# Thirty-four unread products in four places of TensorE's order, in a post-norm attention and ternary FFN kernel

## What is computed

```python
def step(carry, inp):                     # over the 8 segments of 128 tokens
    mem, z = carry
    sq = elu(q) + 1;  att_mem = sq @ mem / (sq @ z)
    sk = elu(k) + 1;  mem = mem + sk^T v;  z = z + sum(sk)
    att = softmax(q k^T * scale) @ v
    return (mem, z), gate * att_mem + (1 - gate) * att
x = layernorm(x + outs @ Wo)
Wq1, Wq2 = quantize(W1), quantize(W2)     # clip(round(W / (mean|W| + 1e-5)), -1, 1)
x = layernorm(x + relu(x @ Wq1.T + b1) @ Wq2.T + b2)
```

## Time and profile before

| | before |
|---|---|
| median of three runs | 1912.11 us (1909.08 to 1915.68) |
| profiled execution | 1912.87 us, its span 1910.9 us |
| TensorE busy | 1855.7 us, 97% of the span, 16575 matmuls |
| VectorE, ScalarE, GpSimd busy | 76%, 53%, 42% |
| mean granted TensorE clock | 0.991 of full speed |

### The profile page before, as it was taken

The page is one execution under the profiler, slowest core; times in us unless marked ns, Lnnn a source line. Parts: engine busy times, 40 slices in busy tenths (PEclk is TensorE's granted clock), DMA queues, the critical chain, the costliest instruction groups (busy, mean ns, idle before and its releaser), DMA issues.

```text
span 1910.9 us, 44707 instructions
## 1 busy us (share of the span) xinstructions
PE 1855.7 (97%) x16575; PEld 1311.8 (69%) x16575; DVE 1449.1 (76%) x2969; ACT 1006.1 (53%) x2426; POOL 794.7 (42%) x790
## 2 busy tenths in 40 slices
PE   5689999999999999999999999999999999999998
PEld 3566677766777766677766677766677766677765
DVE  7867777777777787777777877777777777777774
ACT  5755555555554555554555554545555645555541
POOL 1813344443344444344444344444345444344443
PEclk9889999999999999999999999999999999999999
DMA  8412333223333233233223333323333322333110
GB/s 270 123 23 46 58 61 66 52 49 59 62 59 65 49 53 61 58 60 65 54 45 64 61 59 64 64 38 60 61 59 63 67 38 59 61 58 62 36 23 23
DMA packets 556422, 117.49 MB, mean 61 GB/s; under 512 B 529824, under 2 KB 533808, under 8 KB 555696
## 3 DMA queue, kind: packets, MB, share of 16 engines
q1 hardware_dynamic: 556208, 114.64, 29.4%
HBM read 50.54 MB, written 16.80 MB: 35 GB/s over the span
## 4 chain that ended last, share of the span: by engine, by line
PE 80%; SPq 7%; DVE 6%; DMA 3%; issue 2%; ACT 1%; POOL 1%; DVEq 0%; POOLq 0%; ACTq 0%
PE bank L431 12%; PE bank L430 12%; PE bank L444 8%; PE bank L445 8%; SPq L1551 7%; PE bank L280 6%; PE bank L282 6%; PE bank L281 6%; PE bank L413 3%; PE bank L411 3%; PE bank L412 3%; PE bank L368 3%; DMA amax_row<-amax_dram 2%; PE bank L294 2%; PE bank L347 2%
## 5 line engine op out<-in xcount | busy, mean ns | idle before, releaser
L430 PE MATMUL bank<-yt,w1t 128*128 128x256 f16 x2048 | 453.9, 273 | 0.0
L431 PE MATMUL bank<-yt,w1t 128*128 128x256 f16 x2048 | 453.9, 273 | 0.0
L1141 ACT ACTIVATE prob<-bank,exp_bias,gscalars 128x128 f32<-128x128 f32 x512 | 227.6, 455 | 356.6 <-DVE exp_bias L723 347.7
L444 PE MATMUL bank<-w2t,arena 128*128 128x512 f16 x1024 | 388.4, 379 | 0.0
L445 PE MATMUL bank<-w2t,arena 128*128 128x512 f16 x1024 | 388.1, 379 | 0.0
L1187 ACT ACTIVATE arena<-bank,b_scaled,wscalars 128x256 f32<-128x256 f32 x512 | 262.9, 569 | 213.4 <-PE bank L431 156.3
L858 DVE CAST arena<-arena 128x512 f16<-128x512 f32 x256 | 154.8, 605 | 89.9 <-ACT arena L1187 89.1
L1317 POOL TENSOR_TENSOR att_mem<-att_mem,gate_in 128x512 f32<-128x512 f32 x60 | 83.1, 1385 | 330.1 <-DVE att_mem L762 318.7
L430 PEld LDWEIGHTS bank<-yt,w1t 128*128 128x128 f16 x2048 | 200.5, 98 | 23.3 <-issue 0.3
L431 PEld LDWEIGHTS bank<-yt,w1t 128*128 128x128 f16 x2048 | 200.3, 98 | 22.7
L1395 POOL TENSOR_TENSOR arena<-arena 128x512 f16<-128x512 f32 x128 | 155.3, 1213 | 87.6 <-DVE arena L858 87.6
(11 more groups left out here) (191 smaller groups left out, 4392.9 us busy)
## 6 DMA issues: line engine op xcount, KB each, us to landing
rows<-in_L_attn_x SPq DMA_DIRECT2D x32, 512.0 KB, 3.6
out_rows<-rows SPq DMA_DIRECT2D x64, 256.0 KB, 2.3
x_blocks<-in_L_attn_x SPq DMA_DIRECT2D x248, 64.0 KB, 2.8
sk<-sk_t SPq DMA_DIRECT2D x480, 32.0 KB, 2.0
att_dot<-att_mem SPq DMA_DIRECT2D x480, 32.0 KB, 2.0
y_blocks<-rows SPq DMA_DIRECT2D x480, 32.0 KB
arena<-in_L_ffn_W SPq DMA_DIRECT2D x6, 1024.0 KB, 5.5
w2t<-in_L_ffn_W SPq DMA_DIRECT2D x2, 1024.0 KB, 13.3
```

The lines of the kernel that those rows point to most:

```text
L430: pe.matmul(ps[:, c], w1t[:, k, cols], yt[:, g % 2, :, k], start=k == 0, stop=False)
L431: ins = pe.matmul(ps[:, c], w1t[:, k, cols], yt[:, g % 2, :, KT + k], start=False, stop=k == KT - 1)
L444: pe.matmul(banks[own][:], h_hi[:, f, toks], w2t[:, f, :], start=f == 0, stop=False)
L1141: ins = act.activation(prob[:, t, at], ps[:, c], ACT.Exp, scale=gcol(g, G_EXP), bias=exp_bias[:, t, at:at + 1], accum_out=row_sum[:, t, h: ...
```

## The change

A new function `warm(n)` issues n matmuls of the identity `ident16` with `w_hi["k"][:, 0, :]`, 128 x 512 in float16, each one overwriting all of bank 1. Nothing reads what they write, and they wait for nothing and signal nothing. They are called in the pass g = 0 alone, at four places: 14 between `turn_max(3)` and `scores(0, 0)`, 8 between `sum_all(1)` and `turn_p(0, 0, 1)`, 6 between `turn_p(0, 0, 1)` and `turn_p(0, 1, 0)`, and 6 between `turn_p(0, 1, 0)` and `turn_p(0, 1, 1)`.

```diff
+            def warm(n):
+
+                for _ in range(n):
+                    pe.matmul(banks[1][:], ident16[:], w_hi["k"][:, 0, :], start=True, stop=True)
+
...
                 if g == 0:
                     turn_max(3)
+                    warm(14)
                 ffn_up(g - 2, 7)
...
                 if g == 0:
                     sum_all(1)
+                    warm(8)
                 ffn_down(g - 2, 1, 1)
                 turn_p(g, 0, 1)
+                if g == 0:
+                    warm(6)
                 turn_p(g, 1, 0)
+                if g == 0:
+                    warm(6)
                 turn_y(g - 1, 0)
                 turn_p(g, 1, 1)
```

## The result

| | before | changed |
|---|---|---|
| median of 7 runs | 1911.29 us (1909.08 to 1915.68) | 1918.75 us (1915.25 to 1924.01) |
| ratio | | 1.0046, 95% interval 1.0029 to 1.0063 |
| span of the profiled execution | 1910.9 us | 1921.3 us |

The profiled execution of the change is at the slow end of its runs (1923.31 us). Three of the seven lie there, at 1923.3 to 1924.0 us with a mean granted clock of 0.990; the other four take 1915.3 to 1918.8 us at 0.992. The profile tells where time can go, and only the runs tell how much on average.

The account below looks back on a forecast made before the run. TensorE was taken to bound the kernel, busy for 97% of the span, with only the chain before 131 us movable. Terms 0 + 0 - 0.6 us took the median of 1912.11 to 1911.5 us, range 1908 to 1916 us.

Parts of the forecast that it names:

- Price of a product, first place: The 14 products before `scores(0, 0)`: 0.216 us each at full clock, 3.0 us hidden in the `q_lo` wait, net 0.
- Second to fourth place: The 8, 6 and 6 around `turn_p`: clock rises at 57 us, `turn_w(0)` no later than 62.09 us, path cost 0.
- The rival by which the products are paid at the lower clock and push `turn_w` back: If the clock rises only after 65 us, the chain from `turn_w(0)` is 2.9 us late: 1915.0 us; chance 0.15.
- The late outcome: With transposes counting as pauses for the clock, the time would be nearer to 1915.0 than to 1911.5 us.
- What the full clock brings there: `turn_w(2)` 0.45 us earlier for VectorE, GpSimd's compares 0.7 us earlier, net gain 0.6 us at the last `turn_y`.
- 93% of the time is out of reach of products that are issued before 62 us: From 131 us TensorE is busy 1766.3 of 1779.9 us at full clock; added products only move when that stretch begins.
- TensorE full from 131 us with the same busy time: A sign expected in the changed profile: the stretch from 131 us stays full, its busy time unchanged.
- The sum and the range: 0 + 0 - 0.6 us, from the median of 1912.11 to 1911.5 us (-0.03%); range 1908 to 1916 us.
- The chance of 0.04 for slower by over 0.3%: Chance given to a loss over 0.3% (5.7 us), as run scatter on top of an outer case.
- the three rivals: Nothing gained (chance 0.27), late by up to 2.9 us (0.15), more than forecast, 2.7 us gained (0.08).

Follow-up runs that it names:

- pad34: Kernel before plus 34 one-column products in TensorE's idle first 18 us, none at the four places: 1925.86 us against 1917.73, ratio 1.0038.
- pad64: Kernel before plus 64 one-column products (128 instructions) in TensorE's idle first 18 us: 1928.48 us against 1917.73, ratio 1.0058.
- pad96: Kernel before plus 96 one-column products (192 instructions) in TensorE's idle first 18 us: 1915.93 us against 1912.14, ratio 1.0014.
- change_plus94: Changed kernel plus 94 one-column products in TensorE's idle first 18 us, 256 added instructions in all: 1917.86 us against 1917.73 before, ratio 0.9999.
- pad128: Kernel before plus 128 one-column products (256 instructions) in TensorE's idle first 18 us: 1917.44 us against 1917.73, ratio 1.0000.

## Why the prediction was wrong

By the steps of the prediction:

- **Price of a product, first place.** Right: 3.18 us at the full clock (3.0 forecast), hidden, the clock full until 51.2 us, no gain on the path, the clock low again before `scores(0, 1)`.
- **Second to fourth place.** Right: the rise came at 58.0 us (57 taken), the 8 ended at about 57 us, `turn_w` was not late. The rival by which the products are paid at the lower clock and push `turn_w` back did not happen. By the rule that the prediction cites from the Trainium skill, TensorE: Matmul & The Clock Gate, Part 4, transposes do not count as work towards the full clock. The late outcome that the prediction drew from it did not come either: the rise was at 58.0 us. No run isolates transposes, though, since 8 ordinary products stood before the rise, so the rule itself is neither shown nor refuted.
- **What the full clock brings there.** Right in place and size: `sum_all(2)` 0.5 us sooner counted from `turn_max(3)` (0.45 forecast), the last `turn_y` 90.98 in place of 91.85 us after it, 0.87 us (0.6 forecast). The other half microsecond of the 1.35 is that `turn_max(3)` came earlier in that execution, at 34.90 us in place of 35.38 us.
- **"93% of the time is out of reach of products that are issued before 62 us", and "TensorE full from 131 us with the same busy time".** This step failed, and with it the forecast. The sum had a term missing: 68 instructions more in TensorE's stream. I asked what the products occupy and who waits behind them, not what they move by being code. In the profiled execution the term was 5.6 us of gaps (13.1 - 7.5) and, by difference, some 6 us for 13.6 us at half the clock, which could cost 6.8 us at most; with the 1.35 us the other way that makes the 10.4 us between the spans. Over the runs the medians moved by 7.5 us, and the term is that and the local gain. Pad34, the same 68 instructions without the products, cost 0.38%, against 0.46% for the change.
- **The sum and the range.** 1911.5 us forecast, 1918.75 measured, above the range's 1916. The chance of 0.04 for slower by over 0.3% rested on scatter; none of the three rivals named the mechanism.

What could have warned me stood in the trace of before: gaps of 1.0 and 1.3 us before `attend` in a stage that I took as full, moves of 12 to 14 us among moves of 9.8 us, and an instruction queue in the page's table of queues. The Trainium skill, Runtime: NRT & Kernel Launch, section Instruction fetch mechanics, says that instruction memory is refilled in blocks of 16 KiB, 256 instructions, through DMA. The runs agree: packets of queue 8 have 16384 bytes, and 256 added instructions cost nothing (ratio 1.0000) while 68 do (1.0038), and so do 128 (1.0058), though the latter not through the moves. The page also calls the cost of a block boundary mostly hidden; here some 0.4% of the time hangs on where the boundaries fall, and the measurement stands.

**What stays open.** Why a load of code that takes 0.9 to 1.4 us elsewhere holds up SyncE's issues for up to 3.7 us when it meets them: that they coincide is shown for every issue over 1 us, what they share is not. The load is drawn out too when it meets a move, to 2.9 us in the median of before against 1.1 us elsewhere. Groups 6, 12 and 13 are the worst in the changed kernel, and there a second load, of queue 14, falls into the same moves (at 800.13 us in group 12, that of queue 8 at 803.62 us). It lies 2.2 us behind the start of the move in group 6 of both kernels, so it seems to go with SyncE's own instructions, which is an inference from its place. Why the clock falls in some executions of a kernel and not in others was not tested. What pad64 and most executions of pad96 lose, and whether change_plus94 keeps the local gain, stays open as said above.

## What to carry to other kernels

An instruction that costs nothing where it stands can still move every later load of its engine's code, as the 34 small products of pad34 did here. In a long unrolled kernel a difference of a few tenths of a per cent after an edit near the start should be tested against the same count of idle instructions at a harmless place, and against a filling up to 256, before it is put down to the edit. Better than hunting for a lucky count is slack: taking three `p_split` out from behind the block moves gave 0.54% (1904.56 us, the fastest version here), more than the added products gained or lost. It did not make the kernel insensitive: the same 68 instructions cost the reordered kernel 0.38% too.

## What was not expected of the hardware

- Code comes in pieces of 16384 bytes on queue 8, 135 of them in the changed kernel. They move with TensorE's instructions: 68 more cost 0.38% and 256 more 0.00%.
- A DMA issue of SyncE that takes 0.611 us in the median took up to 4.316 us while such a piece was under way, in the changed kernel.
- After gaps of 2.34 and 2.50 us TensorE ran 6.8 us each at 1.2 GHz though it was busy on both sides; after 1.89 us, in the same execution, it did not. So a wait of 2.4 us cost up to 3.4 us more. The length of the gap alone does not decide: the clock fell for 6.8 us after 1.98 us in pad34, and for 3.4 us after gaps of 0.92 and 0.40 us in pad128, but not after one of 1.64 us in change_plus94.
